# Paged attention: cached keys and values staged per kv group in DRAM, one gather each per sequence, keys turned on VectorE

## What is computed

```python
B, S, HID = 8, 128, 512            # D = 128, HQ = 32 query heads, HK = 8 kv groups
q = rope(rmsnorm(x @ Wq.T, q_norm_w), pos)
k = rope(rmsnorm(x @ Wk.T, k_norm_w), pos);  v = x @ Wv.T
kc = k_cache[block_table].reshape(8, 512, 8, 128)   # 16 pages of 32 keys per sequence
vc = v_cache[block_table].reshape(8, 512, 8, 128)   # caches: (64 pages, 32, 8 groups, 128) f32
# masked softmax of q against 512 cached keys (those below cache_len) and the 128 own keys,
# 4 query heads per kv group; then @ Wo.T, then the feed-forward part, added to x
```

## Time and profile before

| | |
|---|---|
| time, median of 3 runs | 1505.8 us (1503.9 to 1505.9) |
| profiled execution: its own time | 1504.12 us |
| profiled execution: span | 1502.2 us |
| PE busy | 1465.0 us (98%) |
| DVE busy | 1205.7 us (80%) |
| ACT busy | 873.8 us (58%) |
| POOL busy | 989.8 us (66%) |
| SP's transfers (queue q1) | 263536 packets, 97.57 MB, 27.9% of 16 DMA engines |
| POOL's gathers (queue q0) | 16384 packets, 33.59 MB, 7.7% |

### The profile page before, as it was taken

One profiled execution on the slowest core, in us unless ns is written; L12 is line 12 of the kernel. 1 busy time (PEld: TensorE's weight loads), 2 busy tenths in 40 slices (PEclk: granted clock), 3 DMA queues, 4 the chain that ended last, 5 costly groups with the idle time before them and its releaser, 6 DMA issues.

```text
span 1502.2 us, 26807 instructions
## 1 busy us (share of the span) xinstructions
PE 1465.0 (98%) x8600; PEld 1249.9 (83%) x8600; DVE 1205.7 (80%) x2694; ACT 873.8 (58%) x2272; POOL 989.8 (66%) x1297
## 2 busy tenths in 40 slices
PE   8899999989999999999999999999999999999997
PEld 7788888778888888888888888888888888888885
DVE  3788887678888888888888888888888878887865
ACT  3432332366666667666666666666666666666631
POOL 1463432267778787877777788777777878766521
PEclk9999999999999999999999999999999999999999
DMA  7888855232232223233322332232223223321102
GB/s 230 181 205 191 182 127 157 69 83 66 64 80 67 68 68 79 67 77 73 71 64 68 75 75 67 68 86 69 65 64 80 68 66 70 101 60 50 52 15 84
DMA packets 281066, 133.37 MB, mean 89 GB/s; under 512 B 237912, under 2 KB 247512, under 8 KB 280928
## 3 DMA queue, kind: packets, MB, share of 16 engines
q1 hardware_dynamic: 263536, 97.57, 27.9%
q0 software_dynamic: 16384, 33.59, 7.7%
q10 hardware_dynamic: 1008, 0.50, 0.1%
HBM read 107.47 MB, written 7.34 MB: 76 GB/s over the span
## 4 chain that ended last, share of the span: by engine, by line
PE 83%; POOL 7%; issue 4%; DVE 3%; ACT 2%; DMA 1%; POOLq 0%; SPq 0%; DVEq 0%
PE ps_t L1046 11%; PE ps_o L803 10%; PE ps_o L805 9%; PE ps_o L804 9%; PE ps_b L803 5%; PE ps_b L804 5%; PE ps_b L805 5%; PE ps_q L805 3%; PE ps_q L803 3%; PE ps_q L804 3%; PE ps_a L803 3%; PE ps_a L805 3%; PE ps_a L804 3%; PE ps_a L875 3%; POOL vraw L653 2%
## 5 line engine op out<-in xcount | busy, mean ns | idle before, releaser
L1557 ACT ACTIVATE sm<-sm,mn 128x640 f32<-128x640 f32 x256 | 211.0, 825 | 210.3 <-DVE mn L2061 210.3
L1926 DVE TENSOR_TENSOR pT_lo<-ps_t,pT_hi 128x512 fp32r<-128x512 f32 x320 | 220.1, 688 | 99.1 <-ACT pT_hi L1474 98.9
L1474 ACT ACTIVATE pT_hi<-ps_t 128x512 fp32r<-128x512 f32 x320 | 188.6, 589 | 82.8 <-PE ps_t L1046 82.7
L1046 PE MATMUL ps_t<-ident,sm 128*128 128x128 f32 x1280 | 196.4, 276 | 3.5 <-DVE qT_lo L1926 2.1
L1046 PEld LDWEIGHTS ps_t<-ident,sm 128*128 128x128 f32 x1280 | 148.4, 141 | 51.2 <-DVE qT_lo L1926 19.4
L653 POOL DMA_INDIRECT kraw<-in_L_cond_k_cache_dram,idx_a x128 | 130.7, 1021 | 55.6 <-issue 43.3
L653 POOL DMA_INDIRECT kraw<-in_L_cond_k_cache_dram,idx_b x128 | 130.6, 1020 | 51.9 <-issue 47.0
L696 POOL TENSOR_TENSOR z<-pairs_p,zl 128x128 f32<-128x128 f32 x160 | 57.9, 401 | 153.5 <-DVE pairs_p L1779 153.5
L653 POOL DMA_INDIRECT vraw<-in_L_cond_v_cache_dram,idx_b x128 | 131.5, 1027 | 31.5 <-issue 27.6
L653 POOL DMA_INDIRECT vraw<-in_L_cond_v_cache_dram,idx_a x128 | 131.1, 1024 | 30.9 <-issue 27.6
L803 PE MATMUL ps_o<-pT_lo,v_hi 128*128 128x512 f32 x320 | 125.6, 393 | 0.0
(11 more groups left out here) (272 smaller groups left out, 4421.4 us busy)
## 6 DMA issues: line engine op xcount, KB each, us to landing
fv<-st SPq DMA_DIRECT2D x128, 128.0 KB, 2.4
tab<-tab_scratch SPq DMA_DIRECT2D x64, 256.0 KB
wblk<-n_L_attn_weight_qkv_dram SPq DMA_DIRECT2D x24, 384.0 KB, 6.2
wpraw<-_L_attn_weight_proj_dram SPq DMA_DIRECT2D x8, 1024.0 KB, 6.0
mask<-mask_scratch SPq DMA_DIRECT2D x64, 128.0 KB
wtile<-in_L_cond_Wq_dram SPq DMA_DIRECT2D x112, 64.0 KB
wtile<-in_L_cond_Wo_dram SPq DMA_DIRECT2D x112, 64.0 KB
wraw<-n_L_attn_weight_qkv_dram SPq DMA_DIRECT2D x2, 1536.0 KB, 13.6
```

The costliest lines, as they stand in the source:

```text
L1046: mm = pe.transpose(ps_t[bank][:, o * P:(o + 1) * P], i, ident[:])
L1474: act.activation(dst, src, ACT.Copy).then_inc(t_hi, 1)
L1557: act.activation(sm[:, h, :], sm[:, h, :], ACT.Exp, bias=mn[:, h:h + 1], scale=-1.0, accum_out=den[:, h:h + 1]).then_inc(e_done, 1)
L1926: dve.tensor_tensor(lo, src, hi.bitcast(F32), ALU.subtract).then_inc(t_lo, 1)
```

## The change

For each kv group, SP copies that group's keys and values of all 64 pages into two scratch arrays in DRAM: keys as `[half page][block c of 32 dims][16 keys][32 dims]`, values as `[half page][q][u][128]`, both double buffered by g. The rows of the scratch arrays are 2 KB. POOL then issues one gather of 128 rows of 2 KB for the keys of a sequence and one for its values, in place of four and four. The gathered keys lie in 32x32 blocks; one VectorE block transpose makes the transposed keys of a step from them, ACT makes the high part and POOL the low part. The K group leaves PE, its bank, and DVE's and ACT's chain on it. The order of the cached keys within a step changes; the mask's key numbers (`keyidx`) follow it. Core of the diff, by stream:

```diff
-        kraw = at("kraw", [P, 2, KC, P], F32, 188)
+        kblk = at("kblk", [P, 2, CACHED], F32, 188)
+        kT_turn = at("kT_turn", [P, 2, KEYS], F32, 128)      # the place of kT_lo
 # SP, at the start, behind load_wp(1)
+            sp.dma_start(part[:], part_d).then_inc(pages_in, 16)
+            for i in range(8):
+                sp.dma_start(pages[16 * i:16 * i + 16, :], table_pages.rearrange("n m -> m n"),
+                             allow_slow_non_contiguous=True).then_inc(pages_in, 16)
 # SP
+            def stage_k(g, c):
+                sp.dma_start(kst_d[g % 2][:, c, :, :],
+                             k_cache[:, :, g, c * 32:(c + 1) * 32].rearrange("a (f j) e -> (a f) j e", f=2)
+                             ).then_inc(kst_in[g % 2], 16)
+            def stage_v(g, q):
+                sp.dma_start(vst_d[g % 2][:, q, :, :],
+                             v_cache[:, :, g, :].rearrange("a (f u q) d -> (a f) u q d", f=2, q=4)[:, :, q, :]
+                             ).then_inc(vst_in[g % 2], 16)
 # SP, first block: behind load_wp(6) and behind load_wp(7)
+                if g == 4:
+                    for i in range(4):
+                        stage_k(0, i)
+                if g == 5:
+                    for i in range(4):
+                        stage_v(0, i)
 # SP, step (g, n): behind the step's weight tiles, ahead of the tables
+                if not last and n < 4:
+                    if n == 0 and g >= 1:
+                        for i in range(2):
+                            wait_alone(sp, kg_in[i], g * 4 * 16)
+                            wait_alone(sp, vg_in[i], g * 4 * 16)
+                    stage_k(g + 1, n)
+                    stage_v(g + 1, n)
 # POOL
+            def gather_k(g, n):
+                pool.indirect_dma_start(kblk[:, n % 2, :], None, kst_d[g % 2].rearrange("a c j e -> (a c) (j e)"),
+                                        bass.IndirectOffsetOnAxis(idx[:, n:n + 1].bitcast(U32), 0)
+                                        ).then_inc(kg_in[n % 2], 16)
+            def k_low(J):
+                wait_alone(pool, k_hi, J + 1)
+                pool.tensor_tensor(kT_lo[:, J % 2, 0:CACHED], kT_turn[:, J % 2, 0:CACHED],
+                                   kT_hi[:, J % 2, 0:CACHED].bitcast(F32), ALU.subtract).then_inc(k_lo, 1)
 # POOL, step
+                if n == N - 2 and not last:
+                    wait_alone(pool, kst_in[(g + 1) % 2], ((g + 1) // 2 + 1) * 64)
+                    wait_alone(pool, vst_in[(g + 1) % 2], ((g + 1) // 2 + 1) * 64)
-                    gather(k_rows, kraw, kg_in, idx, (n + 2) % N, par)
+                    wait_alone(pool, k_turned, J + 1)
+                    gather_k(g2, n2)
...
                 pool.tensor_tensor(v_lo[:, KC, :], kvown[:, 1, :], v_hi[:, KC, :].bitcast(F32), ALU.subtract
                                    ).then_inc(vs_lo, 1)
+                if not (last and n == N - 1):
+                    k_low(J + 1)
...
-                    gather(v_rows, vraw, vg_in, idx, (n + 2) % N, par, range(KC - 1))
+                    gather_v(g2, n2)
                 if not (last and n == N - 1):
                     stats_k(J + 1, 1 - par)
-                if more:
-                    gather(v_rows, vraw, vg_in, idx, (n + 2) % N, par, range(KC - 1, KC))
 # PE, step
                         pe.wait_ge(s_read, J * 4 + h + 1)
+                        if h == 0:
+                            pe.wait_ge(k_lo, J + 1)
...
-                    k_group(*idx("K"), g + (n == N - 1), n1)
 # ACT, step: group("K") becomes copy_k(J + 1)
+            def copy_k(J):
+                act.wait_ge(k_turned, J + 1)
+                act.activation(kT_hi[:, J % 2, 0:CACHED], kT_turn[:, J % 2, 0:CACHED], ACT.Copy).then_inc(k_hi, 1)
 # DVE
+            def turn_k(J):
+                g, n = J // N, J % N
+                dve.wait_ge(kg_in[n % 2], (g * 4 + n // 2 + 1) * 16)
+                dve.transpose(kT_turn[:, n % 2, 0:CACHED], kblk[:, n % 2, :]).then_inc(k_turned, 1)
 # DVE, step: behind normalise(1)
+                if nxt:
+                    turn_k(J + 1)
                 if tiles:
                     turn(tiles[0])
                 if not (first and n < 1):
                     output_lo(J)
-                if nxt:
-                    group("K")
```

More of the change, by code:

```diff
@@ L35 @@
 PAGE = 32
+PAGES = 64
 CACHED = 512
@@ L186, in block_program @@
         halfs = at("halfs", [P, HG + 1], F32, SM + 0.5)
-        idx_a = at("idx_a", [P, N * KC], I32, SM + 0.53125)
-        idx_b = at("idx_b", [P, N * KC], I32, SM + 0.65625)
-        slot8 = at("slot8", [P, 1], I32, SM + 0.78125)
+        idx = at("idx", [P, N], I32, SM + 0.53125)
+        part = at("part", [P, 1], I32, SM + 0.78125)
         kvown = at("kvown", [P, 2, P], F32, SM + 0.8125)
@@ L205, in block_program @@
         mask_d = nc.dram_tensor("mask_scratch", [N, P, CACHED], BF16, kind="Internal").ap()
+        part_d = nc.inline_tensor(np.array([4 * (p // 16 % 2) + p // 32 for p in range(P)], np.int32).reshape(P, 1), "gather_parts").ap()
+        kst_d = [nc.dram_tensor(f"kst{i}_scratch", [2 * PAGES, 4, 16, 32], F32, kind="Internal").ap() for i in range(2)]
+        vst_d = [nc.dram_tensor(f"vst{i}_scratch", [2 * PAGES, 4, 4, P], F32, kind="Internal").ap() for i in range(2)]
         freq_d = nc.inline_tensor(inverse_frequencies().reshape(1, 64), "rotary_freqs").ap()
         b_rows = lora_b.rearrange("a r i -> (a r) i")
-        k_rows = k_cache.rearrange("a s g d -> (a s g) d")
-        v_rows = v_cache.rearrange("a s g d -> (a s g) d")
         x_in = [sem(f"x_in{i}") for i in range(N // 2)]
@@ L287, in block_program @@
         tab_in = [sem(f"tab_in{i}") for i in range(2)]
+        kst_in = [sem(f"kst_in{i}") for i in range(2)]
+        vst_in = [sem(f"vst_in{i}") for i in range(2)]
+        k_turned = sem("k_turned")
+        k_hi = sem("k_hi")
+        k_lo = sem("k_lo")
         kg_in = [sem(f"kg_in{i}") for i in range(2)]
@@ L638, in _, with gather_indices, gather_v @@
                              ).then_inc(aj_ok, 1)
[L639 to L655, removed]
+            def gather_indices():
+                pool.wait_ge(pages_in, 16 * 9)
+                pool.tensor_scalar(idx[:], pages[:], 8.0, None, ALU.mult).then_inc(idx_ok, 1)
+                pool.wait_ge(idx_ok, 1)
+                pool.tensor_tensor(idx[:], idx[:], part[:].broadcast_to([P, N]), ALU.add).then_inc(idx_ok, 1)
+                pool.wait_ge(idx_ok, 2)
+            def gather_k(g, n):
+                pool.indirect_dma_start(kblk[:, n % 2, :], None, kst_d[g % 2].rearrange("a c j e -> (a c) (j e)"),
+                                        bass.IndirectOffsetOnAxis(idx[:, n:n + 1].bitcast(U32), 0)
+                                        ).then_inc(kg_in[n % 2], 16)
+            def gather_v(g, n):
+                pool.indirect_dma_start(vraw[:, n % 2, :, :].rearrange("p u d -> p (u d)"), None,
+                                        vst_d[g % 2].rearrange("a q u d -> (a q) (u d)"),
+                                        bass.IndirectOffsetOnAxis(idx[:, n:n + 1].bitcast(U32), 0)
+                                        ).then_inc(vg_in[n % 2], 16)
             def tables():
@@ L705, in _ @@
                     masks()
-                if g == 3:
+                if g == 2:
+                    gather_indices()
+                if g == 5:
                     pool.wait_ge(tab_out, 32 * N)
[L708 to L711, removed]
+                    pool.wait_ge(kst_in[0], 64)
+                    for n in range(2):
+                        gather_k(0, n)
+                if g == 6:
+                    pool.wait_ge(vst_in[0], 64)
+                    for n in range(2):
+                        gather_v(0, n)
             def stats_k(J, par):
@@ L729, in stats_q @@
                 pool.tensor_scalar(qs[:, par, :], rs[:, par, 0:HG], -SCALE, None, ALU.mult).then_inc(st_done, 1)
+            def k_low(J):
+                wait_alone(pool, k_hi, J + 1)
+                pool.tensor_tensor(kT_lo[:, J % 2, 0:CACHED], kT_turn[:, J % 2, 0:CACHED],
+                                   kT_hi[:, J % 2, 0:CACHED].bitcast(F32), ALU.subtract).then_inc(k_lo, 1)
             stats_k(0, 0)
             stats_q(0, 0)
+            k_low(0)
             def step(g, n, last):
@@ L737, in step @@
                 more = not (last and n >= N - 2)
[L738 to L748, removed]
+                g2, n2 = (g, n + 2) if n < N - 2 else (g + 1, n + 2 - N)
+                if n == N - 2 and not last:
+                    wait_alone(pool, kst_in[(g + 1) % 2], ((g + 1) // 2 + 1) * 64)
+                    wait_alone(pool, vst_in[(g + 1) % 2], ((g + 1) // 2 + 1) * 64)
                 if more:
-                    wait_alone(pool, t_full, g * PER_G + PRO + sum(len(groups_of(m, last)) for m in range(n)))
-                    gather(k_rows, kraw, kg_in, idx, (n + 2) % N, par)
-                wait_alone(pool, vg_in[par], (g * 4 + n // 2 + 1) * 64)
```

(6 more changed lines are left out.)

29 lines of the change are left out of this document (10 added, 19 removed).

## The result

The changed kernel takes 1453.7 us (median of 4 runs, 1452.8 to 1455.9) against 1504.9 us (1503.9 to 1505.9) for the kernel before: ratio 0.9664, interval 0.9651 to 0.9677. Forecast were 1464 us in a range of 1455 to 1486.

The account below looks back on a forecast made before the run. PE was taken to bound the kernel, with POOL's order a second bound nearly level. From 1504.1 us, less 28.2 (K group) and 13.7 (lateness), 1462.2; with 1.7 for the median, 1464 us, range 1455 to 1486.

Parts of the forecast that it names:

- PE loses the K group: On PE in attention: 64 groups of four transposes at 0.44 us leave the path, 28.2 us less.
- rival B: Another wait takes PE's freed slot, the lap stays 17.56 us, only POOL's lateness goes: 1492 us; chance 0.07.
- its mirror: PE's slot is gained but lateness stays, kept by something other than gathers: 1478 us; chance 0.04.
- POOL's lateness: On POOL ahead of `stats_k`: fewer gathers remove all ten late steps, 13.7 us less over 55 laps.
- Rival C: On POOL: a gather's cost goes by bytes, 4.1 us, making `stats_k` late every step: 1538 us; chance 0.04.
- The cover of 2.0 us at `stats_k`: On POOL: free at 832.8 with `stats_k` wanted at 834.75; gathers over 3.0 us would use it up.
- `k_lo`, DVE, ACT: PE's added wait for keys' low part has 7.7 us cover; DVE's turn and ACT's copy cost nothing.
- Staging: SP's scratch copies stay hidden: 2.8 us per attention step, 8.8 us in the first block against 12.9 cover.
- the 1469 us that followed: Total if first-block 128 B pieces cost about twice: 17.6 us of copies, 4.7 us past the cover.
- Rivals A and D: First-block staging late, beyond 1472 us, chance 0.08; attention's staged copies far slower, 1748 us at ten times, chance 0.03.
- The sum: Whole kernel: 1504.1 less 28.2 and 13.7 is 1462.2; run median 1.7 above the profiled execution gives 1464 us.

Follow-up runs that it names:

- a_peback: Changed kernel with four identity transposes added on PE in each step where the K group stood, nobody waiting for them; 1483.8 us, ratio 0.9873.
- a_again: Changed kernel, unmodified, run once more for a second profile; 1454.54 us, ratio 0.9681.
- b_onegather: Kernel before with only POOL's gathers changed: one of 2 KB rows each for keys and values, K group kept on PE; 1483.7 us, ratio 0.9877.
- b_again: Kernel before, unmodified, run once more for a second profile; 1502.65 us, ratio 0.9999.
- a_ballast4: Changed kernel with four unused POOL powers of 1.04 us each added ahead of `stats_k` in every step; 1648.8 us, ratio 1.0969.
- b_semsplit: Kernel before, the upper two chunks' gathers counting on four added semaphores, with one more PE wait ahead of each K group; 1507.0 us, one run.

## Why the prediction was right and where it failed

*PE loses the K group: right, 28.2 forecast, 29.3 measured.* `a_peback` against `a_again` gives the slot alone. The chain's 0.44 us was a little short of the 0.47 to 0.48 that one lap gains. The slot is a whole gain because PE alone held the ordinary lap; rival B (1492) and its mirror (1478) are out.

*POOL's lateness: right, 13.7 forecast in 55 laps, 13.5 measured there, 14.4 in all 63* (`b_onegather` against `b_again`). PE's ten waits for `rope_k`, 8.0 us, are gone but for one of 0.2. The gather's cost did go by the number of rows: 1090 and 981 ns on the mean for 2 KB rows, against 1020 for 512 B. Rival C falls. The cover of 2.0 us at `stats_k` reads 2.22 in the trace. Where I was wrong is the price beyond it, which rival C used: 1.15 us per late step was read off steps late by 1.24 us. In `a_ballast4` 1.9 us of lateness cost 2.0 at full clock, which goes with that, but in 46 of 55 laps the lower clock cost 1.56 more.

*`k_lo`, DVE, ACT: right, nothing.* DVE's turn takes 704 ns, ACT's copy 625, POOL's subtraction 1295, as the rows of their kin said. `k_low` ends at 806.1 in the step shown, and no wait of PE names `k_lo`.

*Staging: right, hidden.* In the first block the turn of round 6 starts at 205.30:

```profile
205.30 3.55 DVE L1738 STREAM_TRANSPOSE wT<-wblk 128x768 f32<-128x768 f32 x4
```

That is 2.61 us ahead of the earlier trace rows, and that much the kernel was ahead at the turn of round 1 already; DVE does not wait in front of it. Queue 1 over 165 to 240 us, before:

```profile
q1 hardware_dynamic: 16380, 10.75, 61.7%
```

and after:

```profile
q1 hardware_dynamic: 27197, 13.57, 77.5%
```

10817 packets more in 15.8% of 75 us x 16 engines: 17.5 ns each, where 17.2 was taken from the earlier trace rows. This too is a mix of the keys' 8192 pieces of 128 B, the values' 2048 of 512 B and some others. The changed kernel's queue from 176 to 181 us holds almost nothing but the keys' pieces (5016 of 5133 packets are under 512 B):

```profile
q1 hardware_dynamic: 5133, 0.88, 92.9%
```

That is 14.5 ns each. So a piece of 128 B from DRAM to DRAM costs no more than the small pieces of the earlier trace rows, which land in SBUF. The Trainium skill (DMA: Bandwidth & Descriptors, Specifications) has the engine read, modify and write below 512 B; that this makes a piece twice as dear as one of the earlier trace rows, and the 1469 us that followed, was my own estimate, and these rows contradict it. Whether the engine reads, modifies and writes is not something they show. Rivals A and D fall with it.

*The sum: here it failed.* "Of the profiled execution's own 1504.1: less 28.2, less 13.7, is 1462.2" takes all that is outside the laps as unchanged. It is not: the wait of SP for PE's sequencer at the end fell from 5.0 to 0.2 us. This term was in the trace and I never looked at it; the chain of waits ended for me at the last `fin`. With it the sum would have been 1459, and with the slot at its measured 29.3 it would be 1458, inside the range. The bounds stated for the two terms (0.50 us of slot, 16 us of lateness) lead to 1458 as well and not to the 1455 given, so a time below that needed a term which the sum did not have.

The remaining 4.3 us are small terms. The comparison's runs of before had a median of 1504.9, 0.9 below the one I started from; lateness is 0.7 more over all laps than over the 55; and the profile I summed on reached step 0 2.7 us later than that of `b_again`, by its low-clock stretches. That the median of the runs carries this last term is not shown. On one chip the gain is 48.1 us, and the three measured terms, 29.3 of slot, 14.4 of lateness and 4.9 of end wait, make 48.6.

What is shown and what is only argued: the split into the three terms is shown, each by a kernel that changes it alone or with one other. That the end wait is shorter with fewer gathers is shown at four numbers, two of them by one run each; `b_semsplit` shows that something else moves it too. Why, what PE's sequencer does in that time, and why `b_semsplit` has 6.4 us is open.

## What to carry to other kernels

Before removing work from a nearly level second engine, read its cover at the point that feeds the first one: here two gathers fewer of eight would have bought all 14 us, and the other four only room (2.2 us). Lateness past the cover can cost more than its own length: in `a_ballast4` the gap on PE was mostly followed by matmuls at the lower clock, and 1.9 us of lateness cost 3.6 in 46 laps and 2.0 in nine. And sum from the first instruction to the end of the program: what stands behind the last useful instruction belongs to the sum as well.

## What the runs showed of the hardware that I had not expected

- At the end of the program SP waited for PE's sequencer for 0.2, 0.4, 2.8 and 5.0 us after 128, 256, 384 and 512 indirect DMAs, and for 6.4 us after 512 with four semaphores and a wait per K group more.
- A gather's time on POOL did not depend on the row's size: 963 to 1110 ns by group for rows of 512 B, 1 KB and 2 KB.
- Copies from DRAM to DRAM in pieces of 128 B (with up to a fifth of 512 B) cost 14.5, 16.1 and 17.5 ns per piece and engine in three stretches, about what loads of small pieces cost (17.2 ns).
- With POOL some 1.9 us late in each step, PE stood idle for 1.53 us. In the lap shown it had a granted clock of 0.53 over the 3 us from 709 us; 46 of 55 laps were some 3.6 us longer. In nine laps, one of them behind a gap of the same 1.53 us, the clock stayed at 1.00 and the lap was 2.0 us longer.
